# Second order of a cross-scan layer: reading state products in runs of 16 and writing PSUM through an exchanged view

## The reference

```python
xz = einsum('bhwc,ec->bhwe', x, in_proj_weight); xin, z = split(xz, 2)
x_hw = xc.reshape(Bb, 192, 1024)                       # first order: row by row
x_wh = transpose(xc, (0,1,3,2)).reshape(Bb, 192, 1024) # second order: column by column
xs = each order forwards and backwards                 # 4 directions k
dts, Bs, Cs = projections of xs; delta = softplus(dts + bias)
h = exp(delta * A) * h + delta * Bs * u                # 16 states per channel
y_k = sum over states of h * Cs  + u * Ds
y = y_0 + flip(y_2) + exchange(y_1) + exchange(flip(y_3))   # back to row order
y = norm(y) * silu(z);  out = y @ out_proj_weight.T
```

## Time and profile before

| | |
|---|---|
| median of 3 runs | 3590.24 us |
| lowest and highest | 3587.51 and 3597.89 us |
| the profiled execution's own time | 3596.97 us |
| its span, first to last instruction | 3595.1 us |
| busy: VectorE, GpSimd, TensorE, ScalarE | 83%, 79%, 76%, 56% |
| mean granted clock of TensorE | 0.80 |

### The profile page before, as it was taken

One profiled execution on the slowest core, in us unless ns is written; L12 is line 12 of the kernel. 1 busy time (PEld: TensorE's weight loads), 2 busy tenths in 40 slices (PEclk: granted clock), 3 DMA queues, 4 the chain that ended last, 5 costly groups with the idle time before them and its releaser, 6 DMA issues. The chain is left out here.

```text
span 3595.1 us, 27498 instructions
## 1 busy us (share of the span) xinstructions
PE 2717.0 (76%) x5948; PEld 626.7 (17%) x5948; DVE 2981.3 (83%) x1934; ACT 2027.2 (56%) x2262; POOL 2825.5 (79%) x1212
## 2 busy tenths in 40 slices
PE   5669877887888698245667676778878886988787
PEld 2111111111111111111111112111111111111111
DVE  1899899899989897675988932998999898989994
ACT  3566565657565664313655524656665656656563
POOL 0899999999999997003666613999999999989994
PEclk9778887888788777667789778879887887878787
DMA  2655656473755554103443403574637555555643
GB/s 48 163 136 139 143 137 156 124 169 100 175 137 141 136 144 111 30 0 89 124 107 83 118 1 85 138 172 123 162 107 169 135 138 137 138 138 135 160 121 96
DMA packets 140881, 437.19 MB, mean 122 GB/s; under 512 B 33909, under 2 KB 34619, under 8 KB 140395
## 3 DMA queue, kind: packets, MB, share of 16 engines
q1 hardware_dynamic: 140714, 435.58, 50.1%
HBM read 307.56 MB, written 6.82 MB: 87 GB/s over the span
## 5 line engine op out<-in xcount | busy, mean ns | idle before, releaser
L881 POOL TENSOR_TENSOR L_read<-L_state,L_c_rows 128x1024 f32<-128x1024 f32 x768 | 1799.6, 2363 | 103.2 <-DVE L_state L989 90.0
L671 PE MATMUL L_y_ps<-L_read,L_fold 128*64 128x512 f32 x3072 | 1230.1, 905 | 312.1 <-POOL L_read L881 311.2
L868 POOL TENSOR_TENSOR L_state<-L_du,L_b_rows 128x1024 f32<-128x1024 f32 x256 | 605.3, 2364 | 26.6 <-POOL L_read L881 3.9
L989 DVE TENSOR_TENSOR_SCAN L_state<-L_decay,L_work_ps 128x1024 f32<-128x1024 f32 x256 | 585.3, 2286 | 26.7 <-DVE L_work_ps L970 2.5
L989 DVE TENSOR_TENSOR_SCAN L_state<-L_work_ps,L_state 128x1024 f32<-128x1024 f32 x256 | 581.2, 2270 | 29.8 <-POOL L_state L868 21.3
L814 ACT ACTIVATE L_work_ps<-L_delta,L_a_neg 128x1024 f32<-128x1024 f32 x256 | 286.3, 1118 | 562.4 <-DVE L_state L989 562.3
L989 DVE TENSOR_TENSOR_SCAN L_state<-L_decay,L_row_ps 128x1024 f32<-128x1024 f32 x256 | 585.4, 2287 | 8.8
L814 ACT ACTIVATE L_decay<-L_delta,L_a_neg 128x1024 f32<-128x1024 f32 x512 | 584.3, 1141 | 12.9 <-DVE L_state L989 6.1
L970 DVE TENSOR_TENSOR L_work_ps<-L_du,L_row_ps 128x1024 f32<-128x1024 f32 x256 | 314.3, 1228 | 214.4 <-issue 147.0
L671 PEld LDWEIGHTS L_y_ps<-L_read,L_fold 128*64 128x64 f32 x3072 | 191.2, 157 | 1190.1 <-POOL L_read L881 747.1
L1519 POOL TENSOR_TENSOR L_read<-L_state,L_c_rows 128x1024 f32<-128x1024 f32 x96 | 237.1, 2470 | 165.7 <-DVE L_state L1625 139.5
(11 more groups left out here) (323 smaller groups left out, 2897.7 us busy)
## 6 DMA issues: line engine op xcount, KB each, us to landing
L_b_rows<-L_bc_dram SPq DMA_DIRECT2D x580, 256.0 KB, 4.2
L_c_rows<-L_bc_dram SPq DMA_DIRECT2D x580, 256.0 KB, 4.0
L_delta<-L_delta SPq DMA_DIRECT2D x204, 256.0 KB, 5.9
L_du<-L_du SPq DMA_DIRECT2D x140, 256.0 KB, 6.2
L_du<-L_u SPq DMA_DIRECT2D x64, 256.0 KB, 6.0
L_bc_dram<-L_dbl SPq DMA_DIRECT2D x40, 128.0 KB, 3.4
L_delta<-L_delta_a SPq DMA_DIRECT2D x16, 256.0 KB, 4.4
L_du<-L_du_a SPq DMA_DIRECT2D x16, 256.0 KB, 5.1
```

Source lines behind the costliest of these rows:

```text
L671: m = nc.tensor.matmul(y_ps[i * BLK:(i + 1) * BLK, c, :], fold[:, :], y_half(t, o, i), start=first, stop=last, skip_group_check=True)
L868: nc.gpsimd.tensor_tensor(state[:, last, :], du2[:, d * NBLK + last, :], b_rows[:, g % 2, :], ALU.mult).then_inc(injected_c, 1)
L881: nc.gpsimd.tensor_tensor(read[:, t % READS, :], state[:, t % STATES, :], c_rows[:, g % 2, :], ALU.mult).then_inc(multiplied, 1)
L989: nc.vector.tensor_tensor_scan(state[:, c, way], by[:, way], fed[:, way], 0.0, ALU.mult, ALU.add).then_inc(scanned, 1)
```

## The change

In the second order the state sums no longer exchange where they read but where they write: `y_half` reads `read` with h innermost, 16 contiguous elements and then a step, and the new `y_to` writes the PSUM half as "p w h", with neighbouring elements 32 elements apart. The u side always reads `g_cm` contiguously; for the second order ScalarE writes u through the exchanged view instead. The skip products move from the turn of the second order to that of the first, after the tiles 2, 3 and 4, where they read and write contiguously. The counts of instructions, the semaphores and the tables are otherwise the same.

```diff
-CROSS_SKIP_AT = (0, 1, 2)
+CROSS_SKIP_AT = (2, 3, 4)
...
-            def g_half(image, order, i):
-                img = g_cm[:, bass.ts(image, L)]
-                if order == 0:
-                    return img[:, i * HALF:(i + 1) * HALF]
-                return img.rearrange("p (h w) -> p w h", w=W)[:, i * (W // 2):(i + 1) * (W // 2), :]
+            def g_half(image, i):
+                return g_cm[:, bass.ts(image, L)][:, i * HALF:(i + 1) * HALF]
...
             def y_half(t, o, i):
-                src = read[:, t % READS, :] if isinstance(t, int) else t
                 if o == 0:
-                    return src[:, i * HALF:(i + 1) * HALF]
-                return src.rearrange("p (w h) -> p h w", h=H)[:, i * (H // 2):(i + 1) * (H // 2), :]
+                    return read[:, t % READS, i * HALF:(i + 1) * HALF]
+                return read[:, t % READS, :].rearrange("p (w h) -> p w h", h=H)[:, :, i * (H // 2):(i + 1) * (H // 2)]
+
+            def y_to(c, o, i):
+                to = y_ps[i * BLK:(i + 1) * BLK, c, :]
+                return to if o == 0 else to.rearrange("p (h w) -> p w h", w=W)
...
                     for i in range(2):
-                        m = nc.tensor.matmul(y_ps[i * BLK:(i + 1) * BLK, c, :], fold[:, :], y_half(t, o, i),
+                        m = nc.tensor.matmul(y_to(c, o, i), fold[:, :], y_half(t, o, i),
                                              start=first, stop=last, skip_group_check=True)
                     m.then_inc(y_added, 1)
-                    if o == 1 and t in CROSS_SKIP_AT:
+                    if o == 0 and t in CROSS_SKIP_AT:
                         k = CROSS_SKIP_AT.index(t)
...
-                                             y_half(u[rows:rows + BLK, j, :], o, i), start=False, stop=False,
+                                             u[rows:rows + BLK, j, i * HALF:(i + 1) * HALF], start=False, stop=False,
...
-                    ins = nc.scalar.copy(u[:, j, s], side_ps[:, :])
+                    if turn.next_order == 0:
+                        ins = nc.scalar.copy(u[:, j, s], side_ps[:, :])
+                    else:
+                        turned = u[:, j, :].rearrange("p (w h) -> p h w", h=H)[:, i * (H // 2):(i + 1) * (H // 2), :]
+                        ins = nc.scalar.copy(turned, side_ps[:, :].rearrange("p (h w) -> p h w", w=W))
```

More of the change, by code:

```diff
@@ L609, in side @@
                 if kind == "u":
-                    parts = [(w_u[:, j * 128:(j + 1) * 128], g_half(turn.next_image, turn.next_order, i))]
+                    parts = [(w_u[:, j * 128:(j + 1) * 128], g_half(turn.next_image, i))]
                 elif kind == "bc":
@@ L621, in side @@
                 elif kind == "z":
-                    parts = [(w_z[:, j * 128:(j + 1) * 128], g_half(turn.done_image, 0, i))]
+                    parts = [(w_z[:, j * 128:(j + 1) * 128], g_half(turn.done_image, i))]
                 elif kind == "shift":
```

## The result

The changed kernel takes 3565.33 us, the median of 17 runs (3559.98 to 3577.80), against 3585.16 us for the kernel before, also of 17 runs (3576.63 to 3597.89). The ratio is 0.9949, interval 0.9938 to 0.9959: faster by 18.3 us, between 15 and 22. The forecast was 11 us less on a median of 3590.24 us, from three runs; so of the 14 us between 3579 and 3565, about 5 are that median, which more runs put at 3585.16, and about 7 are the effect itself (most of what is left is that the ratio isn't quite that of the two medians).

The account below looks back on a forecast made before the run. The prediction took GpSimd to set the pace in the turns, VectorE close behind. Its terms, -13 - 2 + 3 + 1 = -11 us, took the median 3590.24 to 3579 us, range 3562 to 3594.

Parts of the forecast that it names:

- rival 4: Tile 35 of the second order: the sums shift TensorE's clock there favourably, -17 us more, 3562 us; chance 0.07.
- The bound: In the turns GpSimd sets the pace with fixed work; only its idle time, 78.4 and 50.3 us, can be won.
- The skip products leave the second order: TensorE's queue ahead of the u sides: three sets a turn go, GpSimd's waits for the sums vanish, -13 us.
- Side effects of shorter sums: Sides queued behind a sum on TensorE at the high clock end 0.85 us sooner; -2 us, ends 0 and -17.
- The sums write exchanged: Second-order sums writing PSUM with a step cost nothing extra; bounds nothing to 0.85 us a tile.
- Rival 1: Second-order sums: the exchanged write costs what the read did, 1.8 us a tile at the high clock; 3581 us; chance 0.16.
- rival 3: Second-order sums: PSUM's exchanged write becomes a bound, 3.6 us a tile, 491 us more, 4081 us; chance 0.13.
- The skip products enter the first order: Sets ahead of the cent sides delay VectorE and GpSimd 0.5 us in six turns, +3 us; ends 0 and +35.
- Rival 2: First order: the moved skip products bring their 13 us stall along, 2.2 us a turn; 3589 us; chance 0.14.
- u: contiguous read 0, exchanged write +1: First-order turns: TensorE's faster u sides worth nothing; ScalarE's 48 exchanged copies, up to 0.46 us each, mostly covered, +1 us.
- The signs given: L671 near 770 ns, its wait under 2 us, TensorE about 110 us a second-order turn, L715 0.58 to 1.04 us.

Follow-up runs that it names:

- e1: Kernel before with only the skip products moved to the first order (tiles 2, 3, 4), every view as it was: 3564.78 us, ratio 0.9950.
- e12: Repeat of e1, skip products alone moved against the kernel before, run beside e11: 3567.27 us, ratio 0.9951.
- e4: Kernel before with the skip products of the cross layers left out altogether: 3567.92 us, ratio 0.9958.
- e3: Kernel before with only u of the second order changed, g read contiguously and ScalarE writing u exchanged: 3585.33 us, ratio 1.0003.
- e11: The changed kernel repeated, measured against the kernel before: 3562.57 us, ratio 0.9945.
- e9: The changed kernel with u as before, so skip products moved and new views of the sums: 3566.09 us, 0.9951 of the kernel before.
- e8: The changed kernel with 96 added matmuls per cross layer, fp32 or bf16, writes and reads in order or exchanged: 3759.30 us in one execution.
- e2: Kernel before with only the second-order sums changed, read in runs of 16 and PSUM written exchanged: 3577.43 us, ratio 0.9972.
- e7: The changed kernel with three overwritten matmuls in TensorE's wait ahead of the second order's third sum side: 3560.88 us, 0.9936 of the kernel before.
- e5: The changed kernel with the second order's third sum side at tiles 34 and 35 instead of 32 and 34: 3563.61 us, 0.9942 of the kernel before.
- e6: The changed kernel with first-order sums reading exchanged but writing in order: 3598.76 us, 1.0042 of the kernel before.

## Why the prediction was right, and where it was off

The direction and the range held, and the largest term was the right one. The range held in part by luck: its low end, 3562, stood for rival 4, a stall at tile 35 that would dissolve of itself. It didn't; 3565 lies 14 us under the forecast of 3579 and within 3 of that end. About 5 of the 14 are the median of the kernel before. By its own steps:

**The bound.** GpSimd sets the pace. This holds: TensorE lost 254 us of work and the kernel 18 us. That GpSimd's work is fixed, and that the change touches none of it, doesn't hold: its busy time in the second order fell by 7.5 us, since its product takes 12 ns less beside the new read. The forecast has no term for this.

**The skip products leave the second order: -13.** Right in place and mechanism, and short in size. The waits named (0.38 and 1.42 us in the turn at 600.8) are gone, and e1 alone takes the direct wait for the sums from 13.0 to 0.4 us. (In e12, which repeats e1, it is 3.3 us, of which 0.8 are in the second order.) But e1 wins 18 us (interval 11 to 25) and e4, which has no skip products anywhere, 15 (10 to 20). This is the mis-sized step, together with the term for the first order below: the forecast counted only the idle time that ends with L671. By that count the term was lucky, too: 13.0 us is what the one profiled execution of 3596.97 us shows, and e3, with the skip products in their old place, shows 8.8. In e1 and e12 the gaps of GpSimd that end with VectorE are shorter as well, 90.0 to 79.9 and 79.7 us; a late sum may come back later as a wait for something else. But in e3, whose time didn't move, these gaps are 73.8 us. So where the missing 2 to 5 us lie stays open; they are within the intervals.

**Side effects of shorter sums: -2.** No run shows such an effect: with the skip products gone, GpSimd's idle time in the second order is 52 to 58 us with slow sums (e1, e12, e4) and 57 to 66 with the new views (the changed kernel, e11, e9). What the fast sums bring there is the pace of GpSimd's product, 12 ns on each of 384 products and 14 on each of 128 of GpSimd's injections (L868) in the second order: 384 x 12 + 128 x 14 = 6400 ns or 6.4 us. The turns of the second order are 7 to 8 us shorter in the profiles of the changed kernel and e11 than in those of e1 and e12, and the medians of e11 and e12 lie 4.7 us apart; e9 and the other medians don't show it. Whether the kernel keeps the 6.4 us stays open.

**The sums write exchanged: nothing.** Right, and for the reason given, if in other words: 0.95 ns an element in pairs is the fp32 pace, and the write needs no more. Rival 1 (as dear as the read) and rival 3 (a bound at 3.6 us a tile) fall with the 1.94 us for two tiles and with e8. The Trainium skill says in "PSUM — Partial Sum Buffer", Specifications, that a non-contiguous pattern slows matmuls significantly. Here the measurement decides: in fp32 it doesn't at all, at either clock (0.429 and 0.854 us against 0.429 and 0.853); in bf16 it does, by a factor of two (0.854 against 0.427 at 0.50).

**The skip products enter the first order: +3.** It was 0 as far as the medians tell: e4 wins no more than e1. The step took 1.97 us a set, from the kernel before, and asked what of it fits into 1.26 us of idle time. In fact the sets take 1.08 in the turn shown, at a clock of 1.00 where there was 0.56, and a matmul of a set takes 732 ns in the mean in the changed kernel, e1, e11 and e12, against 1076 in the old place. The cent sides behind them run at 616 ns instead of 853, and VectorE's wait for the last cent fell by 4.8 us instead of rising. That the clock comes from the filled gap is what the windows suggest, and it isn't shown: the two cent sides take 728 and 729 ns in e1, with the sets, and 638 and 784 in e4 and 675 and 658 in e2, without them there, and VectorE's wait is 9.0, 6.6 and 6.8 us. (The lower price that the step gave for a set, 0.85 us, isn't in the rows either; four contiguous instructions take 0.97 in the earlier trace rows.) Rival 2 falls with e4: without any sets the first order's idle time of GpSimd is no shorter, 52 us against 48 and 50 in e1 and e12.

**u: contiguous read 0, exchanged write +1.** Right: e3 is at 1.0003. The bound of 0.46 us a copy, taken from VectorE's L301, is also the value: 1044 - 579 = 465 ns. Its cover of 63 us a turn hides it.

**Rival 4, the clock at tile 35.** It didn't come of itself. e7 brings it about and shows that the price was wrong too: the stall goes, more than half of it returns within twelve tiles (9.6 of 17.8 us), because GpSimd then meets VectorE's next late scan, and the time moves by 3 to 6 us.

**The sum.** -13 - 2 + 3 + 1 = -11, measured -18 (-22 to -15). The +3 was 0 and the -13 was -15 to -18; in the place of the -2 stand up to 7 us of GpSimd's own pace. As e1 alone already makes up the 18, the single terms are known no better than their intervals.

The signs given came out so: L671 at 765 ns (near 770); the wait for it at 2.7 us, not under 2 (none of it is left in the second order; all 2.7 are in the first, where there were none before, and as e4 has 2.7 there without the skip products, these aren't shown to be the cause); TensorE at 115.8 us a turn (about 110); the turn at 600.8, now at 602.3, 3.4 us shorter (1.8), 167.2 to 163.8; L715 in the exchanged form at 1044 ns, the upper end of 0.58 to 1.04.

## What to carry to other kernels

Look at what stands in the late engine's queue ahead of the work that somebody waits for, before making that work faster: moving 24 small sets out of a full stretch gave 15 to 18 of the 18 us, and speeding up 1536 matmul instructions on the same engine took no visible idle time off the engine that sets the pace. What these can have brought is up to 7 us, because that engine itself ran 0.5% faster beside them. A moved step is to be priced at the place where it arrives, with the idle time and the clock of that place, not with its duration where it was. And where two engines run in near lockstep, a single stall that is taken away (e5, e7) is in good part met again a few tiles later, so price it at a fraction of its length (here 3 to 6 of 17.8 us).

## What the runs showed of the hardware

- A matmul that writes PSUM with a step of 32 elements needs two array clocks an element. In fp32 that is no loss (0.429 us at 1.00, 0.854 against 0.853 at 0.50), in bf16 it is a factor of two (0.854 against 0.427 at 0.50; e8).
- A matmul that reads SBUF with a step of 32 elements takes 0.86 us for 512 columns in fp32 and in bf16, at 1.00 and at 0.50 (e8). It doesn't follow the array's clock. Read in runs of 16, the fp32 sums take what contiguous ones take, 1.94 us for eight instructions at 1.00.
- TensorE's exchanged read slows GpSimd. The mean of its product in the second order is 2368 ns in the kernel before, 2369 to 2370 in e1 and e12 and 2372 in e3, which all read exchanged there, and 2356 in the changed kernel and in e2. In e6, where the first order reads exchanged, the first order's goes from 2359 to 2370 and the second order's stays at 2354. GpSimd's injection goes with it, 2371 to 2374 ns against 2356 to 2358. That is half a per cent, in each of the kernels that have the read, and on an engine that sets the pace.
- ScalarE's copy of 128x512 fp32 from PSUM takes 1044 ns where it writes SBUF with a step of 32 elements, and 579 contiguous.
